# Expert steps 2 to 16: the second half of the first-layer weights copied by VectorE instead of ScalarE

## What is computed

```python
def block(x, ...):
    x = layernorm(x + attention(x))          # 16 heads of 64, causal
    xn = (x - mean) * rsqrt(var + eps) * gamma + beta
    probs = softmax(xn @ router_w.T / 1.5)    # 8 experts
    w, idx = top_k(probs, 2)
    h = silu(xn @ W1[e])                      # W1[e]: 128 x 512
    y = h @ W2[e]                             # W2[e]: 512 x 128
    return layernorm(x + sum over the two e of w[e] * y[e])
```

## Time and profile before

| | |
|---|---|
| median of 3 runs | 1267.82 us (1267.64 to 1268.97) |
| profiled execution, its own time | 1269.12 us |
| its span, first to last instruction | 1267.4 us |
| granted TensorE clock | 0.999 |
| PE busy | 1242.5 us, 98% |
| ACT busy | 1117.6 us, 88% |
| DVE busy | 1055.6 us, 83% |
| POOL busy | 755.2 us, 60% |

### The profile page before, as it was taken

The page is one execution under the profiler, slowest core; times in us unless marked ns, Lnnn a source line. Parts: engine busy times, 40 slices in busy tenths (PEclk is TensorE's granted clock), DMA queues, the critical chain, the costliest instruction groups (busy, mean ns, idle before and its releaser), DMA issues.

```text
span 1267.4 us, 35998 instructions
## 1 busy us (share of the span) xinstructions
PE 1242.5 (98%) x11032; PEld 1112.4 (88%) x11032; DVE 1055.6 (83%) x5233; ACT 1117.6 (88%) x3468; POOL 755.2 (60%) x1325
## 2 busy tenths in 40 slices
PE   6999999999999999999999999999999899999997
PEld 6888888888888888888888888888888799999996
DVE  7888888888888888888888888888889785558886
ACT  7899999999999988999989999998888798999994
POOL 2246666666555555555555555555555777656776
PEclk9999999999999999999999999999999999999999
DMA  5000000000000000000000000000003333244554
GB/s 215 6 14 23 23 23 23 23 23 23 15 15 15 14 17 17 14 21 17 15 15 15 14 15 14 14 15 14 14 15 148 106 87 87 82 113 143 158 165 136
DMA packets 49356, 60.95 MB, mean 48 GB/s; under 512 B 8320, under 2 KB 35331, under 8 KB 48912
## 3 DMA queue, kind: packets, MB, share of 16 engines
q1 hardware_dynamic: 39520, 41.44, 10.5%
q0 software_dynamic: 8640, 17.13, 4.2%
q10 hardware_dynamic: 1008, 0.08, 0.1%
HBM read 30.72 MB, written 28.81 MB: 47 GB/s over the span
## 4 chain that ended last, share of the span: by engine, by line
PE 92%; ACT 2%; DVE 2%; POOL 2%; issue 1%; DMA 1%; SPq 0%; POOLq 0%; ACTq 0%
PE ps_a L1450 15%; PE ps_s L1493 13%; PE ps_s L1472 11%; PE ps_f L1528 7%; PE ps_b L1485 7%; PE ps_s L1450 7%; PE ps_f L1485 6%; PE ps_b L1744 5%; PE ps_s L1475 4%; PE ps_a L1744 4%; PE ps_b L1450 4%; PE ps_f L1450 3%; PE ps_a L1549 1%; POOL y_tok L753 1%; PE ps_s L1503 1%
## 5 line engine op out<-in xcount | busy, mean ns | idle before, releaser
L789 ACT ACTIVATE f_y<-f_y,neg_max 128x256 f32<-128x256 f32 x512 | 256.3, 500 | 45.6 <-DVE neg_max L1087 45.5
L1087 DVE CUSTOM_DVE_ANT_0 f_y<-ps_s,mask 128x256 f32<-128x256 f32 x512 | 214.7, 419 | 62.7 <-PE ps_s L1475 62.4
L1450 PE MATMUL ps_a<-xt_hi,weights 128*128 128x256 f32 x1024 | 242.5, 299 | 0.0
L678 POOL TENSOR_TENSOR ot_lo<-f_y,ot_hi 128x512 fp32r<-128x512 f32 x128 | 165.0, 1289 | 115.2 <-PE ps_s L1475 109.9
L1103 DVE TENSOR_SCALAR f_y<-f_y,inv_sums 128x256 f32<-128x256 f32 x512 | 195.3, 381 | 7.0
L792 ACT ACTIVATE f_y<-f_y,neg_max 128x128 f32<-128x128 f32 x512 | 199.7, 390 | 0.0
L1493 PE MATMUL ps_s<-ident,f_y 128*128 128x128 f32 x1536 | 195.1, 273 | 0.0
L1450 PEld LDWEIGHTS ps_a<-xt_hi,weights 128*128 128x128 f32 x1024 | 175.1, 189 | 16.0 <-issue 10.6
L753 POOL DMA_INDIRECT y_tok<-f_y,m_dest x142 | 146.3, 1030 | 68.1 <-DVE m_dest L1290 38.5
L1472 PE MATMUL ps_s<-qk 64*128 64x256 f32 x1024 | 176.4, 421 | 6.0 <-ACT pt L837 2.7
L1493 PEld LDWEIGHTS ps_s<-ident,f_y 128*128 128x128 f32 x1536 | 171.8, 141 | 4.8 <-issue 0.3
(11 more groups left out here) (265 smaller groups left out, 3333.5 us busy)
## 6 DMA issues: line engine op xcount, KB each, us to landing
m_x<-queue SPq DMA_DIRECT2D x71, 133.0 KB
f_y<-y_tok SPq DMA_DIRECT2D x32, 256.0 KB, 3.3
queue<-empty SPq DMA_DIRECT2D x8, 532.0 KB, 3.8
x_raw<-in_x SPq DMA_DIRECT2D x32, 128.0 KB
out_x<-f_y SPq DMA_DIRECT2D x15, 256.0 KB, 3.6
y_tok<-f_y,m_dest POOLq DMA_INDIRECT x142
f_y<-in_w SPq DMA_DIRECT2D x1, 2048.0 KB, 11.1
m_w<-in_w SPq DMA_DIRECT2D x1, 2048.0 KB, 15.2
```

Of the source, the lines that this page charges most:

```text
L678: pool.tensor_tensor(ot_lo[:, first:first + 2, :], ot[:, s % 2], ot_hi[:, first:first + 2, :].bitcast(F32), ALU.subtract).then_inc(ot_lo_d ...
L789: act.activation(row[:, 0:2 * P], row[:, 0:2 * P], ACT.Exp, scale=-1.0, bias=neg_max[:, pair, h, 0:1], accum_out=sums[:, d % 2, pair, h, 0:1])
L1087: dve.tensor_tensor_reduce(out=row[:, 0:2 * P], in0=ps_s[:, pair, h, 0:2 * P], in1=mask[:].rearrange("p a b -> p (a b)"), scale=-1.0, scal ...
L1450: ins = pe.matmul(dst, lhs, rhs, start=(i == 0), stop=(i == len(terms) - 1))
```

## The change

In steps 2 to 16 ScalarE copies only the hi half; VectorE copies the lo half, in its iteration j for step j+2, behind `rest_of_x(j+1)` and the activation, ahead of the router and table work. TensorE waits for VectorE's semaphore too. In steps 0, 1 and 17 to 70 ScalarE copies both halves as before. GpSimd's function, which no step reached, goes, and so does the constant.

```diff
-LATER = 71
@@ gpsimd
-            def rest_of_expert_weights(j):
-                if j == NJ1:
-                    pool.wait_ge(table_done, 1)
-                pool.wait_ge(m_z_ready, (j - 1) * 2)
-                col = pool.value_load(tab_w[0:1, j:j + 1], min_val=0, max_val=(E - 1) * HID)
-                pool.tensor_copy(m_w1[:, j % 2, 1], weights[:, bass.ds(col + W1_LO, HID)].bitcast(F32)
-                                 ).then_inc(m_w_lo_done, 1)
-
             for j in range(NJ):
-                if LATER <= j + 2 < NJ:
-                    rest_of_expert_weights(j + 2)
@@ scalar, expert_weights
                 ins = act.activation(m_w1[:, j % 2, 0], weights[:, bass.ds(col + W1_HI, HID)].bitcast(F32), ACT.Copy)
-                if j < LATER:
+                if not 2 <= j < NJ1:
                     ins = act.activation(m_w1[:, j % 2, 1], weights[:, bass.ds(col + W1_LO, HID)].bitcast(F32), ACT.Copy)
                 ins.then_inc(m_w_hi_done, 1)
@@ vector
+            def rest_of_expert_weights(j):
+                dve.wait_ge(m_z_ready, (j - 1) * 2)
+                col = dve.value_load(tab_w[0:1, j:j + 1], min_val=0, max_val=(E - 1) * HID)
+                dve.tensor_copy(m_w1[:, j % 2, 1], weights[:, bass.ds(col + W1_LO, HID)].bitcast(F32)
+                                ).then_inc(m_w_lo_done, 1)
+
@@ vector, the loop over j
                 if j == 0:
                     rest_of_x(1)
+                if 2 <= j + 2 < NJ1:
+                    rest_of_expert_weights(j + 2)
                 if j >= NJ - 2:
                     rows(j - 1)
@@ tensor
             def hidden(j, chunks=range(CH)):
                 pe.wait_ge(m_w_hi_done, j + 1)
-                if j >= LATER:
-                    pe.wait_ge(m_w_lo_done, j + 1 - LATER)
+                if 2 <= j < NJ1:
+                    pe.wait_ge(m_w_lo_done, j - 1)
```

## The result

The changed kernel takes 1272.9 us (median of 6 runs, 1271.91 to 1274.56) against 1268.36 us (median of 6, 1267.53 to 1271.89) for the kernel before, measured beside it: ratio 1.0028, 95% interval 1.0019 to 1.0038. (The ratio of the two medians by themselves would be 1.0036.) It is slower: the whole interval lies above 1, its middle above the 0.2% that counts as a difference here and its lower end just under it. The forecast was 1269.4 us in a range up to 1271.2, with a chance of 0.18 for slower. The profiled execution of the changed kernel took 1273.3 us, of which the span is 1271.5; the profiled one before took 1269.12, span 1267.4. The two spans are 4.1 us apart, and the whole of that must be found.

The account below looks back on a forecast made before the run. TensorE was taken to set the pace; removing ScalarE's copies gained nothing, and six VectorE copies in iterations 6 to 11 less idle and slack added 1.64 us to the median 1267.82: about 1269.4 us, range 1267.2 to 1271.2.

Parts of the forecast that it names:

- The gap at step 16 takes back 1.65.: Before step 16 TensorE's wait, paced by GpSimd's scatter, was taken as slack absorbing 1.65 us of earlier lateness.
- the sum of 1.64 us: Whole change: six copies in iterations 6 to 11, less idle and slack, 6c - 2.44 = +1.64 us.
- The price c: VectorE's added time per copy: 0.38 us copy plus 0.30 exposed register load, 0.68 us, bounded by 0.38 and 0.90.
- The new wait: VectorE's copy for step j+2 waits for step j's first layer, normally done by then; cost nothing.
- the rule: VectorE's SBUF-to-SBUF copy holds the port shared with GpSimd, delaying every overlapped scatter and moving out step 16's gap.
- GpSimd's delay: Scatters met by 12 copies lose 0.7 us, hidden because GpSimd's date at step 16 still lies before TensorE's.
- iterations 0 to 5: cost zero: In iterations 0 to 5 VectorE's idle time and slack hold copies 2 to 7; zero cost, also for GpSimd.
- rival 3: Scatters held for the whole of each of 12 copies: +5.5 us on step 16's gap, 1273.3 us; chance 0.05.
- Rival 2: VectorE becomes the bound of iterations 6 to 11, c 0.90: +2.96 us, 1270.8 us; chance 0.13.
- Rival 1: All hidden: the load hides, c is 0.38 to 0.45, sum 0 to 0.3 us, 1268.0 us; chance 0.23.
- Rival 4: Faster: the 2.16 us scatter finds VectorE free and ScalarE's earlier results close idle; 3 us at most, 1265 us; chance 0.03.

Follow-up runs that it names:

- before_again: The kernel before, unedited, timed and profiled a second time: 1268.92 us against 1268.42, ratio 1.0001.
- before_busy: The kernel before with 18 matmuls on unused results filling TensorE's 2.2 us wait before step 0's transposes: 1270.0 us, ratio 0.9996 to the kernel before.
- only_14_16: The changed kernel with VectorE's copy in steps 14 to 16 alone, ScalarE copying in the others: ratio 0.9997 to the kernel before.
- changed_again: The changed kernel, unedited, timed and profiled a second time: 1273.07 us against 1270.08 for the kernel before, ratio 1.0021.
- no_load: The changed kernel without VectorE's register load, its copy always reading expert 0's weights: 1271.97 us, ratio 1.0027 to the kernel before.
- changed_busy: The changed kernel with 18 matmuls on unused results filling TensorE's wait before step 0's transposes: 1272.67 us, ratio 1.0016 to the kernel before.
- only_8_13: The changed kernel with VectorE's copy in steps 8 to 13 alone, ScalarE copying in the others: ratio 1.0032 to the kernel before.
- load_first: The changed kernel with VectorE's register load put ahead of the subtraction L1304 in the same iteration: 1273.46 us, ratio 1.0029 to the kernel before.
- not_8_13: The changed kernel with VectorE's copy in steps 2 to 7 and 14 to 16 alone, ScalarE copying in 8 to 13: ratio 1.0011 to the kernel before.
- only_4_7: The changed kernel with VectorE's copy in steps 4 to 7 alone, ScalarE copying in the others: ratio 1.0009 to the kernel before.

## Why the prediction was wrong

**Right: what bounds the stage, and where.** VectorE has no idle ahead of L1314 in iterations 7 to 12, the table instruction comes late, TensorE waits for it, the wait before step 16 goes, and from 1059 us nothing is lost or won. L1785 was forecast 3.29 us late and is 3.41. ScalarE's copies bought only longer waits (0.23 us before L899 became 0.73 or more). Steps 14 to 16 cost nothing. That 3.41 lies so near is luck, as shown below.

**The step that failed: "The gap at step 16 takes back 1.65."** In the two executions that were profiled first it nearly did: from the table matmul to step 16 there are 13.98 us before and 12.47 after, so 1.51 came back, and the sum of 1.64 us met a measured 1.94. But the wait of 1.36 us in the earlier trace rows came for the most part from a scatter of 2.16 us that the next executions do not have: before_again, before_busy and only_14_16 have 3.84, 3.69 and 3.85 us between steps 15 and 16, a slack of 0.30 to 0.46. Against before_again the table is 3.45 us late and the gap returns 0.31. The prediction took its sum against the profiled execution, then subtracted the 1.30 us by which the median lies lower, though the two have in part one source: the span of before_again is 1265.2 us, and 1.24 of the 2.2 us between the two spans lie between steps 15 and 16, give or take 0.05. The sum should have been 3.3 - 0.4 = +2.9 us on the median. Measured at step 18: 65.59 and 65.54 against 62.44 and 62.25, about +3.2; changed_again, with its late landing, has 66.52. So the term of the sum that failed is the 1.65 us given back: the runs show 0.31.

The scatter's 2.16 us were a matter of hundredths. It began 0.01 us ahead of L1315, which has the 128x768 operation right behind it; in before_again the twelfth scatter began 0.54 us ahead of L1315 and was not touched. What such a meeting costs can be read from the rows (last section).

**The price c: right in sum, wrong in its parts.** The copy lasts 0.43 us for the estimated 0.46, and adds 0.38 to an iteration (no_load), as taken. The load was put at 0.30 exposed and is about 0.14 in the mean, since only what L1304 does not cover is seen: the copy starts 0.34 to 0.45 us after L1304 where nothing else holds it, not the 0.63 that ScalarE's order suggested. Over the stretch the loss is 21.40 - 18.79 = 2.61 us, which gives c = (2.61 + 0.79) / 6 = 0.57, for 0.68.

**The new wait, "cost at nothing".** Its cover was a first layer that is done by then, and in iteration 8 it was not. The copy for step 10 needs step 8's first layer, whose last matmul starts at 1034.30 and lasts 0.28; the load runs behind that wait, and so in full. The copy starts 0.77 us after L1304, with 0.34 us of idle on VectorE that is marked "issue", and the iteration takes 4.31 us for 3.48 (of which 0.18 were idle). The profile has four such idles: iterations 0, 8, 13 and 14; only that of iteration 8 lies where VectorE has nothing to spare.

**GpSimd, and the rule.** The prediction put GpSimd's delay at 0.7 us and called it hidden, since it looked only at the gap before step 16. The 0.8 us that the copies of steps 4 to 7 cost it is not hidden at step 7. So "iterations 0 to 5: cost zero" holds for VectorE and fails by way of GpSimd: at the table matmul 0.80 from step 7 and 2.61 behind it make the 3.41. Two errors, of +0.68 and -0.80, met in a total that looked exact. Part of the 2.61 is something that the sum had no term for: the copy of 0.70 us in iteration 10, 0.27 over the others, in the changed kernel, changed_again, changed_busy and only_8_13 alike. Of rival 3 the mechanism is there but not the size: GpSimd's instructions are held when they begin beside a copy, and of the 18 scatters that start from 1023 to 1046 us 13 take the usual 0.98 to 1.00. The Trainium skill (SBUF — State Buffer, section "SBUF: two separate sides") has VectorE and GpSimd lock each other out of a shared port for a whole instruction. The trace agrees in part: L637 ends nearly as the copy beside it does (1016.79 + 0.49 against 1016.81 + 0.41), L607 does not (1013.32 + 0.93 against 1013.27 + 0.42), and of the 18 scatters none begins inside a copy, while three have a copy begin inside them and still take 0.98 to 1.00 us (1023.07, 1035.06 and 1043.03, with copies at 1023.94, 1035.34 and 1043.56).

**Rival 2** (VectorE as the bound, +2.96 us, 1270.8 us) came nearest in size. It asked for c of at least 0.83, however, and c is 0.57: the loss came with the smaller price because the slack was missing. **Rival 1** asked for a c near 0.38, which no_load has; even so the table matmul would be 6 x 0.38 - 0.79 = 1.5 us late. **Rival 4**'s scatter of 2.16 us is gone from the later profiles, of both kernels alike, so nothing is gained by it.

**The rest up to the medians.** The medians are 4.54 us apart beside the first pair of profiles, 2.99 in changed_again, 2.67 with the clock kept up. The recorded ratio of the first comparison, 1.0028, is 3.6 us. What its medians have beyond 3.2 us fits half clock before step 1 in some of its runs: the changed profile lost 2.18 us that way, and three of the six runs have a mean clock of 0.996 (1273.04 to 1274.56 us), three 0.998 (1271.91 to 1272.76). Why one execution has it and another not stays open.

## What to carry to other kernels

A slack that is read off one wait in one execution, above all one paced by another engine's transfers, is not there to spend: read the same gap in a second execution of the unchanged kernel before it goes into the sum. Move work to the engine that idles in the very iterations concerned, not to the one whose share of the span is lower (VectorE 83%, ScalarE 88%): 14 to 16 were free, 8 to 13 cost most of it. Where the time goes to waiting for a buffer, more buffers pay more than moved work: two more result buffers gave 0.9986 (0.9976 to 0.9997).

## What the runs showed of the hardware

- A register load from SBUF on VectorE's sequencer took 0.31 us in the median of 15 (0.30 to 0.55) and its arithmetic 0.19 us more. Behind one operation of 128x256 about 0.14 us of it was exposed in the mean, behind operations of 0.15 us mostly 0.15 to 0.33 us (load_first, idle before L1304; 0.63 once), and behind a wait 0.34.
- The copy of 128x512 between fp32r tiles in SBUF took 0.43 us. One in iteration 10 took 0.70 (1043.56), again in three other profiles; a scatter was under way at its start, but so it was beside copies of 0.43, and no run takes that apart.
- What a scatter lost to VectorE can be read from the rows: it was the time from 0.12 us after its start to the end of the VectorE operation then running, for L1304 or L1315 and for the 128x768 operation. At 1025.26 L1315 ended 0.42 us after the scatter's start and the scatter was 0.29 over its 0.98; the 2.16 of 1034.62 was 1.18 over, and the 128x768 operation ended 1.30 after its start; in before_again (1034.56) it was 0.42 over for 0.53, in the changed kernel (1038.97) 0.16 over for 0.29. Operations that began 0.11 us or more after the scatter did not hold it (1043.03, 0.98 us, L1304 at 1043.14). It is an estimate from such rows, and it fails where the two begin almost together: in the changed kernel a scatter that began 0.02 us after a copy (1058.42) took 0.98, and the copy 0.48 for 0.43; in before_again one that began 0.01 us ahead of L1315 (1024.25) took 0.98, and L1315 0.45 for 0.42; in only_14_16 one that met the same pair of operations as the scatter of 2.16 us, at 1034.81, took 1.25.
- TensorE's granted clock fell to half after a wait of 2.2 us in some executions, and not in others with the same wait:

```profile
990.25 0.44 PE L1546 MATMUL ps_a<-ident,m_x 128*128 128x128 f32 x2 [2.23 <-DMA m_x<-queue]
```

```profile
990.11 0.44 PE L1549 MATMUL ps_a<-ident,m_x 128*128 128x128 f32 x2 [2.20 <-DMA m_x<-queue]
```

  The first is the changed kernel, at half clock for the next stretch and 2.18 us later at step 1; the second the kernel before, at full clock. Filling the wait with matmuls kept the full clock in both profiles so made, and the mean granted clock of 12 timed runs each at 0.9986 and 0.9988 against 0.9970 unfilled. It gained nothing that can be measured on the kernel before (0.9996). A stretch below full clock stands between 985 and 998 us in seven of nine profiles of kernels in which VectorE makes some of the copies of steps 4 to 13, and in none of the five others; the mean clocks of the timed runs (0.9974 and 0.9970 on the chip of changed_again) don't bear that pattern out, and most of those copies lie behind the stretch. It is left open.
- From the second scatter of step 0 to the L1314 that waits for its landing there were 2.36 to 2.39 us in seven of the profiles and 2.88 to 3.37 in four others (changed_again, only_8_13, not_8_13, only_4_7). It moves step 7 by about 1 us (24.88 and 25.99 in two executions of the changed kernel), and nothing here explains it.
